# Order of the last output products, and the last result in two halves, in a two-layer attention block

## What is computed

```
x = x + ga * linear_attention(modulated_norm(x))
h = modulated_norm(x)
for e in range(4):                       # 512 tokens each
    m = 256 >> e                         # 256, 128, 64, 32 channels
    out_e = attn_out_e[..., :m] @ o_w[:m, :m].T + o_b[:m]
x = x + gb * (concat(pad(out_e)) + h)
```

## Time and profile before

| | |
|---|---|
| median of 3 runs | 1831.88 us (1831.05 to 1836.23) |
| profiled execution | 1832.7 us, span 1830.6 us |
| mean granted TensorE clock | 0.969 of full |
| TensorE busy | 1712.8 us, 94% of the span |
| VectorE busy | 1396.4 us, 76% |
| GpSimd busy | 1140.8 us, 62% |
| ScalarE busy | 1101.3 us, 60% |
| the last result L1228, 128x1024 | 1.22 us, once a batch |
| stores of `X` to the output | 16 of 512 KB |

### The profile page before, as it was taken

One profiled execution on the slowest core, in us unless ns is written; L12 is line 12 of the kernel. 1 busy time (PEld: TensorE's weight loads), 2 busy tenths in 40 slices (PEclk: granted clock), 3 DMA queues, 4 the chain that ended last, 5 costly groups with the idle time before them and its releaser, 6 DMA issues.

```text
span 1830.6 us, 31834 instructions
## 1 busy us (share of the span) xinstructions
PE 1712.8 (94%) x11538; PEld 979.6 (54%) x11538; DVE 1396.4 (76%) x2617; ACT 1101.3 (60%) x2066; POOL 1140.8 (62%) x1062
## 2 busy tenths in 40 slices
PE   6999899999899989999979998999988999899997
PEld 4776544444577554444357754444436775444443
DVE  5887877776588788777668878777757878777774
ACT  2885536666488544666658853466656875356664
POOL 2783457667578345766758724776685862477665
PEclk8999989999899999999999999999998999899999
DMA  5000450010200045001110005300111001620101
GB/s 181 2 2 1 141 144 10 18 44 12 81 2 2 1 152 133 14 14 44 35 59 2 1 33 171 82 19 13 41 58 35 2 2 55 184 55 10 50 4 46
DMA packets 56011, 89.54 MB, mean 49 GB/s; under 512 B 13224, under 2 KB 31912, under 8 KB 53036
## 3 DMA queue, kind: packets, MB, share of 16 engines
q1 hardware_dynamic: 54704, 87.45, 16.4%
q10 hardware_dynamic: 1152, 0.07, 0.0%
HBM read 49.29 MB, written 35.72 MB: 46 GB/s over the span
## 4 chain that ended last, share of the span: by engine, by line
PE 68%; DVE 12%; ACT 8%; POOL 5%; issue 3%; DMA 2%; SPq 2%; ACTq 0%; POOLq 0%; DVEq 0%
PE PS L1449 14%; PE PS L1634 13%; PE PS L1622 11%; PE PS L1647 6%; PE PS L1347 5%; PE PS L1355 3%; PE PS L1372 3%; PE PS L1382 3%; DVE MXP L1059 2%; ACT HT L631 2%; ACT HTR L634 2%; DVE STAT L952 2%; ACT PR L852 1%; DVE QKS L1128 1%; PE PS L1498 1%
## 5 line engine op out<-in xcount | busy, mean ns | idle before, releaser
L594 POOL TENSOR_TENSOR TS<-PR 128x1024 f32<-128x1024 f32 (+1 forms) x256 | 573.3, 2239 | 301.7 <-ACT PR L852 235.6
L1059 DVE TENSOR_REDUCE MXP<-PS 128x1 f32<-128x512 f32 x960 | 600.1, 680 | 179.6 <-PE PS L1449 179.0
L852 ACT ACTIVATE PR<-PS 128x512 f32<-128x512 f32 x960 | 503.0, 602 | 357.0 <-PE PS L1622 348.2
L1449 PE MATMUL PS<-KOP,QOP 96*128 96x512 f32 x960 | 420.1, 450 | 9.9 <-DVE MXP L1059 4.8
L1622 PE MATMUL PS<-QOP,KOP 97*128 97x512 f32 x960 | 377.2, 406 | 14.9 <-ACT PR L852 11.5
L1449 PEld LDWEIGHTS PS<-KOP,QOP 96*128 96x128 f32 x960 | 185.6, 194 | 276.2 <-DVE MXP L1059 214.2
L1634 PE MATMUL PS<-PR,V 128*32 128x512 f32 x1920 | 276.1, 609 | 0.0
L1622 PEld LDWEIGHTS PS<-QOP,KOP 97*128 97x128 f32 x960 | 180.7, 191 | 78.2 <-ACT PR L852 45.9
L1647 PE MATMUL PS<-TS,ones 128*32 128x512 f32 x960 | 133.2, 593 | 5.4 <-POOL TS L594 5.4
L514 POOL TENSOR_SCALAR PK<-XSK 128x1024 f32<-128x1024 f32 x64 | 67.0, 1047 | 98.7 <-ACT XSK L690 98.4
L1382 PE MATMUL PS<-PB,QKT 64*128 64x256 f32 x1536 | 127.0, 298 | 1.4 <-DVE VE L946 1.0
(11 more groups left out here) (152 smaller groups left out, 2634.0 us busy)
## 6 DMA issues: line engine op xcount, KB each, us to landing
KOP<-k_scr SPq DMA_DIRECT2D x84, 256.0 KB, 5.5
k_scr<-QKS SPq DMA_DIRECT2D x64, 256.0 KB, 2.9
QOP<-q_scr SPq DMA_DIRECT2D x180, 64.0 KB, 2.0
q_scr<-QKS SPq DMA_DIRECT2D x40, 256.0 KB, 2.9
X<-in_L_attn_x_dram SPq DMA_DIRECT2D x16, 512.0 KB, 4.9
out_dram<-X SPq DMA_DIRECT2D x16, 512.0 KB, 3.1
QOP<-MXT SPq DMA_DIRECT2D x224, 0.5 KB
KOP<-QKS SPq DMA_DIRECT2D x36, 64.0 KB, 2.0
```

What stands on the lines that cost most here:

```text
L594: g.tensor_tensor(sums(k)[:, 0:len(stage)], pair[:, :, 0], pair[:, :, 1], ALU.add).then_inc(S["psum_t"], 1)
L852: a.activation(PR[:, k % 2, w, q], bank(score_bank(p, n, w, q)), ACT.Exp).then_inc(S["ex"], 1)
L1059: v.tensor_reduce(MXP[:, u % 2, i, kc:kc + 1], bank(max_bank(p)), AX.X, ALU.max).then_inc(S["am_rd"], 1)
L1449: mm(bank(max_bank(p)), QOP[0:96, u % QS6, i * P:(i + 1) * P], KOP[0:96, h % KS6, kc * CH:(kc + 1) * CH], start=True, stop=True).then_inc( ...
```

## The change

TensorE's `last_output` is split by operand. The first-operand products of all four quarters are done in a row, ahead of the next batch's `project`; the second-operand products of all four follow behind `project_values`. Since two quarters share a bank, only the first of the two begins it. TensorE signals after the second and after the fourth quarter on a semaphore of its own, `ops_last`. VectorE adds the result in two halves of two quarters each (`last_result`), and SyncE stores each half (256 KB) by itself, with the next batch's load of the slot before between the two stores.

```diff
--- before.py
+++ after.py
@@ -221,7 +221,7 @@
                    ve2 rs3 rstd2 ve3 nmr3 h2 x2 x2T xn_sb qp q_hi q_lo scr0 scr1 scr2 vp v2_sb vb_ok obm
                    q_in0 q_in1 q_in2 q_in3 q_in4 q_in5 kf0 kf1 kf2 kf3 k_in1 k_in2 k_in3 k_in4 k_in5 k_in6 k_in7
                    one_set one_st k_one am am_rd top top_ps top_sb mxt shift0 shift1 shift2 shift3 shift4 shift5
-                   sc_b ex pv psum_t den2 cs_up c_out pool_own rcp at at_last base ops fin st0 st1 st2 st3 fin_n dve_own""".split()
+                   sc_b ex pv psum_t den2 cs_up c_out pool_own rcp at at_last base ops ops_last fin st0 st1 st2 st3 fin_n dve_own""".split()
         S = {n: sem(n) for n in names}
         q_in = [S[f"q_in{i}"] for i in range(QS6)]
         shift = [S[f"shift{i}"] for i in range(QS6)]
@@ -418,22 +418,30 @@
                         for h in range(KS6, H2N):
                             load_k(h)
 
-                for k, e in enumerate(results):
+                for k, e in enumerate(results[:-1]):
                     s = slot_of[e]
-                    sp.wait_ge(S["fin"], NC * b + k + 1)
+                    sp.wait_ge(S["fin"], (NC + 1) * b + k + 1)
                     sp.dma_start(ov[:, bass.ds(b * NC + e, 1)].rearrange("p o t d -> p (o t) d"),
                                  X[:, slot(s)]).then_inc(st[s], 16)
                     if k > 0 and not last:
                         wait_all(sp, (st[slot_of[results[k - 1]]], 16 * (b + 1)))
                         load_x(b + 1, slot_of[results[k - 1]])
+                s = slot_of[0]
+                for h in range(2):
+                    sp.wait_ge(S["fin"], (NC + 1) * b + NC + h)
+                    sp.dma_start(ov[:, bass.ds(b * NC, 1), 2 * h:2 * h + 2].rearrange("p o t d -> p (o t) d"),
+                                 X[:, s * TPC + 2 * h:s * TPC + 2 * h + 2]).then_inc(st[s], 16)
+                    if h == 0 and not last:
+                        wait_all(sp, (st[slot_of[results[-2]]], 16 * (b + 1)))
+                        load_x(b + 1, slot_of[results[-2]])
                 if not last:
-                    wait_all(sp, (st[slot_of[results[-1]]], 16 * (b + 1)))
-                    load_x(b + 1, slot_of[results[-1]])
+                    wait_all(sp, (st[s], 32 * (b + 1)))
+                    load_x(b + 1, s)
 
             for b in range(B):
                 batch(b, b == B - 1)
             for s in range(NC):
-                sp.wait_ge(st[s], 16 * B)
+                sp.wait_ge(st[s], (32 if s == slot_of[0] else 16) * B)
 
 
         @block.gpsimd
@@ -1223,9 +1231,17 @@
                 e = results[k]
                 s, m = slot_of[e], width[e]
                 src = out_ps(e).rearrange("p (t d) -> p t d", t=TPC)
-                dve.wait_ge(S["ops"], b * NC + k + 1)
+                dve.wait_ge(S["ops"], b * (NC - 1) + k + 1)
                 dve.wait_ge(S["base"], 2 * (b * NC + k + 1))
                 v.tensor_tensor(X[:, slot(s), 0:m], src, X[:, slot(s), 0:m], ALU.add).then_inc(S["fin"], 1)
+
+            def last_result(b, h):
+
+                s = slot_of[0] * TPC + 2 * h
+                dve.wait_ge(S["ops_last"], 2 * b + h + 1)
+                dve.wait_ge(S["base"], 2 * NC * b + 2 * (NC - 1) + h + 1)
+                v.tensor_tensor(X[:, s:s + 2], out_ps(0)[:, 2 * h * D:2 * (h + 1) * D].rearrange("p (t d) -> p t d", t=2),
+                                X[:, s:s + 2], ALU.add).then_inc(S["fin"], 1)
 
             def begin(b):
                 dve.wait_ge(S["x_first"], 16 * (b + 1))
@@ -1250,8 +1266,9 @@
                     part = slice(q * P, (q + 1) * P)
                     v.tensor_tensor(NUM[:, NC, part], NUM[:, NC, part], SUM[:, NC, part], ALU.mult
                                     ).then_inc(S["at_last"], 1)
-                result(b, NC - 1)
-                wait_all(dve, (S["fin"], NC * (b + 1)))
+                last_result(b, 0)
+                last_result(b, 1)
+                wait_all(dve, (S["fin"], (NC + 1) * (b + 1)))
                 if following is not None:
                     begun(following)
 
@@ -1603,7 +1620,7 @@
                     rows = min(m, P)
                     pe.wait_ge(S["am_rd"], NU * MAXU * (b + 1))
                     if k > 0:
-                        pe.wait_ge(S["fin"], NC * b + k)
+                        pe.wait_ge(S["fin"], (NC + 1) * b + k)
                     for i in range(TPC):
                         o = out_ps(e)[:, i * m:(i + 1) * m]
                         last = mm(o, NUM[0:rows, e, i * P:(i + 1) * P],
@@ -1676,24 +1693,27 @@
                 values(SLOTS - 1)
                 denominators(SLOTS // 2 - 1)
 
-                def last_output(i):
+                def last_output(i, k):
                     tok = slice(i * P, (i + 1) * P)
                     o = out_ps(0)[:, i * D:(i + 1) * D]
-                    mm(o, NUM[:, 0, tok], OWG[:, 0], start=True, stop=False)
+                    if k == 0:
+                        return mm(o, NUM[:, 0, tok], OWG[:, 0], start=i % 2 == 0, stop=False, skip_group_check=True)
                     pe.wait_ge(S["at_last"], TPC * b + i + 1)
-                    return mm(o, NUM[:, NC, tok], OWG[:, 1], start=False, stop=True)
+                    return mm(o, NUM[:, NC, tok], OWG[:, 1], start=False, stop=True, skip_group_check=True)
 
                 pe.wait_ge(S["ex"], 2 * NU * STEPS * (b + 1))
                 pe.wait_ge(S["at"], len(RECIPROCALS) * (b + 1))
                 if following is not None:
                     x_transposes(following, 0, 0, 0)
-                last_output(0)
+                for i in range(TPC):
+                    last_output(i, 0)
                 if following is not None:
                     project(following, 0, 0)
                     project_values(following, 0, 0)
-                for i in range(1, TPC):
-                    last = last_output(i)
-                last.then_inc(S["ops"], 1)
+                for i in range(TPC):
+                    last = last_output(i, 1)
+                    if i % 2 == 1:
+                        last.then_inc(S["ops_last"], 1)
                 if following is not None:
                     qk_transposes(following, 0, 0)
                     x_transposes(following, 1, 1, 1)
```

## The result

The changed kernel took 1817.65 us (median of 6 runs, 1814.5 to 1821.79) against 1831.47 us of the kernel before (6 runs, 1830.26 to 1836.23): 13.8 us less, a ratio of 0.9924 with a 95% interval of 0.9912 to 0.9937. Two more groups of runs gave 0.9923 (0.9910 to 0.9937) and 0.9928 (0.9915 to 0.9940). The profiled execution took 1821.6 us (span 1819.5), 11.1 us less than that of before.

A forecast was written before the change was run, and what follows sets the result against it. TensorE, holding 68% of the chain that ended last, was taken as the bound. Boundaries 2.6 us plus program end 1.8 us made 4.4 us off 1831.9, so 1827.5 us, range 1822.5 to 1832.0.

The forecast's parts named there:

- part 1: TensorE's order at the three batch boundaries: two pairs leave the stretch behind `project`, 0.86 us each, 2.6 us in all.
- the two terms of the halves: Program end: VectorE's second half takes 0.69 for 1.22 us, 0.53 less; the last store's halving gives 0.78 us.
- rival D: Split stores push the last load of X over 3.7 us late, VectorE waits; 5 us slip leaves 1831.4 us; chance 0.04.
- Rival C: Another releaser at the transposes or next `project` cancels the boundary gain; only the end gains: 1830.1 us; chance 0.12.
- the 0.5 us for TensorE at the end: Program end: only one pair remains behind VectorE's fourth product, so the result starts sooner; 0.25 to 0.75, taken as 0.5.
- The whole end: Program end: 0.5 from TensorE, 0.53 from VectorE's second half, 0.78 from the store; 1.8 us (0.8 to 2.1).
- My forecast leaves the dips as they are: TensorE's clock drops at the boundaries stay unchanged, booked at nothing; all best would be 9.9 us less, all worst 6.9 more.
- The sum itself: Boundaries 2.6 us plus program end 1.8 us make 4.4 us; chance of the forecast 0.52.
- the sign of this that I had put down: Boundary legs differing by more than the 0.86 us would say the clock, not the order, made the result.
- a gain of over 0.3%: Whole kernel below 1826.4 us, faster than measurement can confuse with no change; chance 0.35.
- rival A: The filled gap ahead of `project` keeps or restores TensorE's clock: 2.9 us more gain, 1824.6 us; chance 0.26.
- rival B: The unbroken idle piece ahead of `project` lengthens the clock dips at every boundary: 2.5 us slower, 1834.4 us; chance 0.06.

The follow-up runs named there:

- fill_only: Kernel before plus first-operand products of quarters 1 to 3 computed once more, unused, ahead of `project` at the three boundaries: ratio 0.9968, 5.9 us faster.
- order_only: Kernel before with only TensorE's `last_output` split by operand as in the changed kernel; one result, one store: ratio 0.9957, 7.9 us faster than before.
- halves_only: Kernel before with its TensorE order kept and only the result and its store split in halves: ratio 0.9993 (0.9985 to 1.0002).
- halves_between: Changed kernel with the halves and two stores at the three boundaries only, one result and store in the last batch: ratio 0.9945 to the kernel before.
- fill_second: Changed kernel plus four unused pairs between the first tile's transposes and the second tile's `project`: ratio 0.9921 to the kernel before, 14.5 us faster.
- fill_more: Changed kernel plus three unused pairs behind the four first-operand pairs in the gap ahead of `project`: ratio 0.9927 to the kernel before.
- less_work: Kernel before with first-operand products of quarters 1 to 3 left out at the three boundaries, results there incomplete: ratio 0.9953, 8.6 us faster.
- order_again: Second measurement of order_only, the kernel before with only TensorE's order changed: ratio 0.9948, 9.5 us faster than before.
- halves_at_end: Changed kernel with the halves and two stores in the last batch only, one result and store at the boundaries: ratio 0.9942 to the kernel before.
- after_again: The changed kernel measured again without edit: 1818.67 us against 1833.74 of the kernel before, ratio 0.9923.
- after_third: The changed kernel measured a third time without edit, as yardstick of its group: ratio 0.9928 to the kernel before, 13.2 us faster.
- fill_both: Changed kernel plus the unused pairs of both fill_more and fill_second: 1816.89 us against 1833.32 of the kernel before, ratio 0.9907.

## Why the prediction was wrong, point by point

**Right.** The six pairs became four and 2.59 us became 1.73. The four pairs ahead fit in the gap even at the slow clock (3.14 us, ended at 921.25, `project` at 922.25). fill_only's first leg less the changed kernel's is 4.94 - 4.08 = 0.86, the step of part 1 exactly, and with the slow clock out of the way. At the end, the two terms of the halves came out: the second half took 0.69 us for 1.22 (0.53, as foretold), and from there to the span's end 0.76 us less passed (0.78 foretold). The load of X kept its cover, so rival D didn't come. Rival C didn't either.

**Right by luck: the 0.5 us for TensorE at the end.** The prediction took them from TensorE being behind at 1824.42 and gave them to the new order. The last result did start sooner, by 0.7 us. But with the order of before and the full clock it starts as soon (0.80 us behind the fourth product in fill_only, 0.79 in the changed kernel). What kept TensorE behind was the slow clock of that one trace (its mean there is 0.50 from 1822 to 1824), and at the full clock the order is worth nothing there. With slow pairs too it is little: order_only's end is 12.9 us, where before had 13.1. The whole end, 2.0 us for 1.8, agrees by that luck; the halves give 1.3 of it, which is the middle of halves_only's interval.

The Trainium skill's page DMA: Bandwidth & Descriptors, Anatomy of one DMA, has its figures for DMAs that GpSimd issues, which the prediction didn't say; here SyncE issues them. Splitting didn't cost. By this trace the store's end moved up by 0.76 us; the page's figures had given 0.6. A single landing scatters as much: the last store of 512 KB landed 2.9 us after its issue before and 3.8 us in halves_between, the last of 256 KB 2.2 us after it in the changed kernel and 3.3 in fill_second.

**The step that failed** is the sentence "My forecast leaves the dips as they are". It put the clock's term at nothing, and the clock in the first legs alone gave 4.2 us. The sum itself held: 2.6 us at the boundaries and 1.3 at the end from the edit, and 0.7 more at the end that were the clock's. The clock, which I had called larger than the sum, did move; the sign of this that I had put down, legs that differ by more than 0.86 us, came at each boundary: the first legs are 2.1, 2.2 and 2.5 us shorter. I had given 0.35 to a gain of over 0.3%.

The direction was that of rival A, and the size was beyond it: I gave A 2.9 us over the first legs. In the traces of the changed kernel the first legs together are 13.8 to 13.9 us, which is 6.8 less than before. 2.6 of that is the order, so 4.2 is the clock.

I held against A that an idle piece of 2.6 us now stands unbroken before `project`, and made rival B of it. At the second and third boundary all seven traces with four pairs in the gap and the rest left alone have `project` at full clock. In seven of these fourteen places the idle piece stood there whole, 2.4 us long; in the other seven the slow clock fell on the pairs and left 0.8 to 1.0 us of it. At the first boundary the piece goes with a slow `project`: the first leg is 5.6 to 5.7 us in all seven. `project` takes 2.01 us in the rows above, where the slow level begins inside it, and 2.70 to 2.93 in the other six. Even so the leg is shorter than the 7.83 of before, as the pairs behind `project` are at the full clock or nearly (1.89 to 2.40 us for four). In fill_second the legs of 5.7 us stand at all three boundaries. With the idle end filled as well (fill_more) the first boundary's leg is 4.16. So B's reason was real, with a price of 1.6 us wherever it struck, but over the three boundaries A's gain is the larger one. Rival B's case, all legs at their longest, came in no trace.

The following table puts the spans of the traces side by side: the first legs and the second legs of the three boundaries, the end of the program from the last product of the denominators (L1647) on, and what lies inside batches 1 to 3, from the key sums to that last product. All in us. Two parts are left out: the 6.1 us from that product to the first `project`, which are the same everywhere (6.3 at two boundaries of fill_more), and the first batch up to there, 468.8 to 473.1 us, in which no kernel here does other work.

| kernel | first legs | second legs | end | inside batches 1 to 3 |
|---|---|---|---|---|
| before | 20.6 | 31.4 | 13.1 | 1276.0 |
| halves_only | 21.2 | 30.1 | 11.1 | 1276.2 |
| fill_only | 14.8 | 31.7 | 12.4 | 1275.8 |
| less_work | 15.5 | 30.2 | 12.4 | 1273.7 |
| order_only | 13.8 | 31.7 | 12.9 | 1274.6 |
| order_again | 13.8 | 30.2 | 12.4 | 1273.5 |
| halves_at_end | 13.9 | 28.7 | 11.6 | 1274.5 |
| halves_between | 13.8 | 28.7 | 13.3 | 1274.8 |
| changed | 13.9 | 30.2 | 11.1 | 1272.9 |
| after_again | 13.8 | 28.7 | 11.1 | 1273.4 |
| after_third | 13.8 | 28.7 | 11.1 | 1272.2 |
| fill_more | 12.4 | 28.7 | 11.1 | 1274.5 |
| fill_second | 17.1 | 27.2 | 12.2 | 1271.7 |
| fill_both | 12.3 | 27.1 | 11.6 | 1274.0 |

Over the three traces of the changed kernel the means are 13.8, 29.2, 11.1 and 1272.8 us. Against before that is 6.8, 2.2, 2.0 and 3.2 us less, 14.2 together, which is the measured 13 to 14. So of the gain 3.9 us are the edit's own work (2.6 at the boundaries, 1.3 at the end), 4.2 us are the clock in the first legs (shown by fill_only), 0.7 us the clock at the end, 2.2 us the clock in the second legs, where spells come at some boundaries and not at others, and 3.2 us lie inside the batches, where the code is the same.

**What stays open** is these last two, 5.4 us together. Each rests on one trace of before (halves_only's, the nearest to it, has 30.1 and 1276.2). The first batch alone, with the same work everywhere, scatters by 4.3 us from trace to trace, more than these 3.2 us. Inside the batches the slow clock is what differs, for instance in these windows of before (columns as in the earlier trace rows, with the instructions of each engine in brackets):

```profile
600.00:650.00 50.00, 46.18 (x350) 27.14 (x342) 37.96 (x111) 24.59 (x44) 14.12 (x24) 0.93 0.05 17
650.00:700.00 50.00, 44.49 (x150) 25.51 (x142) 41.59 (x99) 20.54 (x38) 21.14 (x26) 0.88 0.54 175
```

The same windows after:

```profile
600.00:650.00 50.00, 45.76 (x325) 26.37 (x324) 40.12 (x119) 26.47 (x48) 12.98 (x21) 1.00 0.09 33
650.00:700.00 50.00, 43.02 (x140) 23.09 (x139) 40.19 (x95) 19.01 (x35) 23.34 (x28) 0.93 0.58 179
```

The code of these batches is the same, though the windows don't hold exactly the same instructions (the key sums that begin the batch stand at 495.68 before and at 494.00 after). The mean granted clock is 0.93 and 0.88 in the one and 1.00 and 0.93 in the other. These windows lie in the part that differs most: that batch took 425.8 us before and 422.1 here, but 425.3 and 425.2 in the other two traces of the changed kernel. Why the spells within the batches got fewer was not shown by any run. less_work has part of that gain (2.3 us) without a filled gap and fill_only has none of it (0.2) with one, so it doesn't hang on the fill. A different spacing of the boundaries in time is a possible cause, and it is only argued.

I also took the kernel's scatter too lightly. Single executions of the changed kernel lay between 1814.5 and 1823.6 us, 9 us apart, twice my whole sum. (The ends of the range are also rounded: 1824.6 - 2 is 1822.6 and 1830.1 + 2 is 1832.1.)

## What to carry to other kernels

Where TensorE waits ahead of a block that the critical path runs through, work moved into that wait can be worth more than its own length: the block behind it may run at the other clock level. Here it did at the second and third boundary of all seven such traces, and not at the first. Cost the block behind the gap at both levels from rows of the trace and let that difference into the forecast's middle, not only into a rival. And judge a gap before you fill it by who releases its end: here GpSimd did, so products, even useless ones, cost nothing as long as they ended first. Price them at the slow clock too: seven pairs fit at 0.43 us each, and came 0.2 us late in fill_more where four of them ran slow. And before a slow engine at one place is put down to the order of its work, look for a trace that has the same order at the other clock level.

## What the runs showed of the hardware

Useless work paid. Three pairs of products that nobody reads, at each of three places, made the program 5.9 us faster (ratio 0.9968), and seven pairs at each made the changed kernel about 4 us faster again by the medians (0.9907 against 0.9928, intervals that overlap a little). The slow spell isn't always avoided: in fill_only and in the changed kernel's second boundary it falls on the products in the gap (2.58 us for three pairs, 3.14 for four) and is over when `project` starts. The Trainium skill, TensorE: Matmul & The Clock Gate, What's actually happening, has the rule that activity releases the slow level; with it fill_only agrees, `project` 2.93 us behind a mostly idle gap and 1.65 us behind a filled one at all three boundaries. With four pairs and an idle end it isn't so at every boundary (2.93 us at the first of after_again).

Filling a stretch is no guarantee by itself. fill_second has the same four pairs ahead of `project` as the changed kernel, and all its first legs are 5.7 us, where the changed kernel has 4.1 at two boundaries, while its second legs are all at full clock. Only with both stretches filled were both legs short at all three boundaries. In these traces what a spell costs depends on where it begins, in the gap or on `project`, and that I could not foretell from the rows.
